# Attention of a mixture-of-experts layer: one stream of units, an order for each engine, and scores in two products

## What is computed

```python
x = x + attention(layernorm(x), ctx, mask)     # x 16x224x512, ctx 16x750x384, 8 heads of 64
x = x + ffn(layernorm(x))                      # 8 experts 512 -> 2048 -> 512, top 2, capacity 1120

q, k, v = x @ W_q, ctx @ W_k, ctx @ W_v
sim = where(mask, (q k^T) * 64**-0.5, -max)
out = softmax(sim) v @ W_o + b_o
```

## Time and profile before

| | us |
|---|---|
| median of 3 runs | 2237.76 (2236.44 to 2246.44) |
| the profiled execution | 2237.11 |
| its span | 2235.4 |
| PE busy in the span | 2096.5 (94%) |
| DVE, ACT, POOL busy | 996.3, 678.0, 488.8 |
| attention's logits finished at | 720.93 of the span |

### The profile page before, as it was taken

The page is one execution under the profiler, slowest core; times in us unless marked ns, Lnnn a source line. Parts: engine busy times, 40 slices in busy tenths (PEclk is TensorE's granted clock), DMA queues, the critical chain, the costliest instruction groups (busy, mean ns, idle before and its releaser), DMA issues.

```text
span 2235.4 us, 30763 instructions
## 1 busy us (share of the span) xinstructions
PE 2096.5 (94%) x12038; PEld 1860.0 (83%) x12038; DVE 996.3 (45%) x2223; ACT 678.0 (30%) x1672; POOL 488.8 (22%) x535
## 2 busy tenths in 40 slices
PE   3898998998897699999999999999999999999997
PEld 3777877877875599899989989998998999998997
DVE  4666766666655653422422342242224245234221
ACT  2633634634633222311321131132113124113110
POOL 0643643633633111111010111011111111111100
PEclk9999999999998699999999999999999999999999
DMA  4221121121111332510421251042124225123211
GB/s 131 63 81 50 31 80 44 36 80 38 43 50 57 119 102 64 144 28 19 136 65 15 48 152 36 14 124 70 28 48 137 53 55 154 28 47 115 38 15 15
DMA packets 95528, 148.32 MB, mean 66 GB/s; under 512 B 7920, under 2 KB 49312, under 8 KB 95376
## 3 DMA queue, kind: packets, MB, share of 16 engines
q1 hardware_dynamic: 79632, 109.36, 15.3%
q0 software_dynamic: 15744, 36.71, 9.3%
HBM read 110.66 MB, written 35.39 MB: 65 GB/s over the span
## 4 chain that ended last, share of the span: by engine, by line
PE 65%; DVE 1%; issue 0%; POOL 0%; POOLq 0%; ACT 0%; DVEq 0%
PE psH L1458 31%; PE psY L1458 31%; PE psX L1472 1%; PE psI L1514 1%; DVE w_lo L939 0%; PE psI L1504 0%; POOL out_dram L1274 0%; POOLq L1196 0%; DVE moves L1332 0%; DVE onehot L1340 0%; DVE psH L1410 0%; DVE hT_lo L1436 0%; DVE ys L1380 0%; DVE ys L965 0%; DVE eq_t L1323 0%
## 5 line engine op out<-in xcount | busy, mean ns | idle before, releaser
L1436 DVE SCALAR_TENSOR_TENSOR hT_lo<-psH,hT_hi 128x384 fp32r<-128x384 f32 (+1 forms) x384 | 209.9, 547 | 926.0 <-ACT hT_hi L1299 925.9
L1299 ACT ACTIVATE hT_hi<-psH 128x384 fp32r<-128x384 f32 (+1 forms) x384 | 185.4, 483 | 1112.4 <-PE psH L1458 1112.4
L1458 PE MATMUL psH<-xgT_hi,w_hi 128*128 128x384 f32 (+2 forms) x1536 | 484.3, 315 | 5.6 <-issue 5.4
L1458 PE MATMUL psH<-xgT_hi,w_lo 128*128 128x384 f32 (+2 forms) x1536 | 483.8, 315 | 0.0
L1458 PE MATMUL psH<-xgT_lo,w_hi 128*128 128x384 f32 (+2 forms) x1536 | 482.4, 314 | 0.0
L1458 PE MATMUL psY<-w_hi,hT_hi 128*128 128x512 f32 (+1 forms) x1002 | 403.1, 402 | 0.0
L1458 PE MATMUL psY<-w_lo,hT_hi 128*128 128x512 f32 (+1 forms) x1002 | 394.0, 393 | 0.4 <-issue 0.4
L1458 PE MATMUL psY<-w_hi,hT_lo 128*128 128x512 f32 (+1 forms) x1002 | 394.2, 393 | 0.0
L1458 PEld LDWEIGHTS psH<-xgT_hi,w_hi 128*128 128x128 f32 x1536 | 290.5, 189 | 28.4 <-issue 11.8
L1458 PEld LDWEIGHTS psH<-xgT_lo,w_hi 128*128 128x128 f32 x1536 | 290.6, 189 | 15.4
L1458 PEld LDWEIGHTS psH<-xgT_hi,w_lo 128*128 128x128 f32 x1536 | 290.3, 189 | 0.0
(11 more groups left out here) (188 smaller groups left out, 2939.2 us busy)
## 6 DMA issues: line engine op xcount, KB each, us to landing
stage<-in_L_ffn_W_dram SPq DMA_DIRECT2D x128, 512.0 KB, 4.5
x_sb<-in_x_dram SPq DMA_DIRECT2D x8, 896.0 KB, 7.9
x_res<-in_x_dram SPq DMA_DIRECT2D x8, 896.0 KB, 5.7
out_dram<-x_res SPq DMA_DIRECT2D x8, 896.0 KB, 4.8
xn_rows<-xn SPq DMA_DIRECT2D x8, 896.0 KB, 4.7
c_sb<-in_ctx_dram SPq DMA_DIRECT2D x16, 375.0 KB
out_dram<-zrow SPq DMA_DIRECT2D x9, 256.0 KB, 4.4
xg<-xn_rows,gid POOLq DMA_INDIRECT x72, 3.6
```

Source lines behind the costliest of these rows:

```text
L1299: nc.scalar.activation(hT[0][:, f % 2, 0:m], psH[f % 2][:, 0:m], ACT.Relu).then_inc(h_hi, 1)
L1436: nc.vector.scalar_tensor_tensor(out=hT[1][:, f % 2, 0:m], in0=psH[f % 2][:, 0:m], scalar=0.0, in1=f32(hT[0][:, f % 2, 0:m]), op0=ALU.max, ...
L1458: mm = nc.tensor.matmul(out, stationary(a, c), moving(b, c), start=first and c == chunks[0] and j == 0, stop=last and c == chunks[-1] and ...
```

## The change

Two things change together.

**Scores in two products.** q's hi part is written to both 64-row halves of its head's tile (ACT, two more instructions per `q`); the lo part stays in the head's own half, zeros in the other. k gets a tile for each head (`kz`), with the hi part in the head's own half and the lo part in the other one. Then q_hi over both halves times kz is hi·hi + hi·lo, and q_lo times kz is lo·hi: two matmuls for three. The split of `k` is two 64-row instructions on ACT and on DVE for one each.

**One stream of units.** Units 13 to 15 of a pair (`t-3` to `t-1`, `o-4` to `o-1`), its output projection and its whole tail move into the next pair's iteration, between that pair's units. Each engine gets a table of its own for the first pair, the loop, and the end. The function `iteration` is now called for pair 0, in the loop for 1 to 6, for 7, and once more for the tail of 7. The prologue makes only `fc`, `fx`, `k0` and `q0`; `v0` and `v1` move among the first units, and the weights W_v and W_o are split there (`w7` to `w13`). `tt` uses the ring's banks and no longer `psT`. SP stores the rows of pair p-1 within iteration p and then loads `xr` for pair p; POOL adds the bias late in the iteration, between units 11 and 15. The logits' transpose (`lt`) is a step of its own.

```diff
+PE_STEPS = order("""
+    t-3 q1 s0 k1 o-4 t-2 o-3 s1 s2 t-1 v0 s3 q2 o-2 o-1 t0 wo0 wo1 s4 v1 wo2 t1 v2 o0 v3 s5 o1 tt0 t2 t3
+    s6 s7 tt1 wo3 o2 t4 k2 o3 q3 t5 s8 k3 o4 t6 s9 s10 fc0 o5 tt2 t7 s11 tt3 fx0 o6 fx1 t8
+    s12 lg0 o7 fx2 t9 lt0 s13 o8 fc1 t10 fc2 o9 t11 s14 fx3 s15 k0 q0 o10 o11 t12
+""")
+ACT_STEPS = order("""
+    o-4 t-3 q1 k1 t-2 o-3 s0 v0 t-1 o-2 q2 o-1 s1 t0 s2 v1 s3 o0 v2 t1 v3 o1 t2 s4 s5 t3 s6 o2 t4 k2 o3
...
+""")
+POOL_STEPS = order("""
+    u0 fl0 u1 tl0 tl1 u2 u3 tl2 u4 u5 u6 tl3 u7 u8 u9 u10 u11 bi0 bi1 u12 u13 u14 bi2 bi3 u15
+""")
...
+PRO_ORDER = order("fc0 fc1 fc2 fx0 fx1 fx2 fx3 k0 q0")
...
@@ SP
+            def load_ahead(p):
+                sp.wait_ge(proj_mm, ring_start(p) - 2)
+                load_front(sp, T, A, p + 1)
+                sp.wait_ge(mbias, p + 1)
+                load_mask(p + 1)
+            def rows_out(p, prev, nxt):
+                sp.wait_ge(proj_done, ring(p, prev, nxt, "wo", TP - 1) + 1)
+                sp.dma_start(rows(A["out"][0:NTOK, :], p - 1), xr[:]).then_inc(x2_out, 16)
+                sp.wait_ge(xn2_done, TP * p)
+                sp.dma_start(rows(A["xn2"], p - 1), xn2[:]).then_inc(xn2_out, 16)
+                sp.wait_ge(x2_out, 16 * p)
+                held(sp, passed, xn2_out, 16 * p)
...
             with sp.Fori(1, NPAIR - 1) as p:
-                iteration(p, True)
+                load_ahead(p)
+                rows_out(p, True, True)
+                load_rows(p)
@@ ACT, split_hi
                 elif kind == "q":
-                    nc.scalar.activation(qz[0][0][0:64, i % 2, :], src[0:64, 0:TP * R], ACT.Copy)
-                    nc.scalar.activation(qz[1][0][64:128, i % 2, :], src[64:128, 0:TP * R], ACT.Copy).then_inc(proj_hi, 1)
+                    for h in range(2):
+                        nc.scalar.activation(qz[h][0][own[h], i % 2, :], src[own[h], 0:TP * R], ACT.Copy)
+                    for h in range(2):
+                        a = nc.scalar.activation(qz[h][0][own[1 - h], i % 2, :], src[own[h], 0:TP * R], ACT.Copy)
+                    a.then_inc(proj_hi, 1)
                 else:
-                    nc.scalar.activation(kT[0][:, i % 2, :], src[:, 0:TP * KC], ACT.Copy).then_inc(proj_hi, 1)
+                    for h in range(2):
+                        a = nc.scalar.activation(kz[h][own[h], i % 2, :], src[own[h], 0:TP * KC], ACT.Copy)
+                    a.then_inc(proj_hi, 1)
@@ DVE, split_lo
-                    a, h, o = src[:, 0:TP * KC], kT[0][:, i % 2, :], kT[1][:, i % 2, :]
+                    nc.vector.tensor_tensor(kz[0][64:128, i % 2, :], src[0:64, 0:TP * KC], f32(kz[0][0:64, i % 2, :]), ALU.subtract)
+                    a, h, o = src[64:128, 0:TP * KC], kz[1][64:128, i % 2, :], kz[1][0:64, i % 2, :]
@@ PE
                         for it in range(2):
                             at = b * S + it * R
-                            mm = product(psS[i % 2][0:R, it * NKEY:(it + 1) * NKEY],
-                                         lambda k, c: qz[h][k][:, hp % 2, at:at + R],
-                                         lambda k, c: kT[k][:, hp % 2, b * NKEY:(b + 1) * NKEY], 1)
+                            for k in range(2):
+                                mm = nc.tensor.matmul(psS[i % 2][0:R, it * NKEY:(it + 1) * NKEY], qz[h][k][:, hp % 2, at:at + R],
+                                                      kz[h][:, hp % 2, b * NKEY:(b + 1) * NKEY], start=k == 0, stop=k == 1,
+                                                      skip_group_check=True)
```

More of the change, by code:

```diff
@@ L159 @@
[L159 to L185, removed]
@@ new lines @@
+""")
+ACT_STEPS = order("""
+    o-4 t-3 q1 k1 t-2 o-3 s0 v0 t-1 o-2 q2 o-1 s1 t0 s2 v1 s3 o0 v2 t1 v3 o1 t2 s4 s5 t3 s6 o2 t4 k2 o3
+    s7 q3 t5 k3 s8 o4 fc0 t6 o5 t7 s9 fx0 fx1 t8 s10 s11 fx2 t9 o6 s12 fc1 fc2 o7 t10 t11 fx3 o8 o9
+    s13 k0 o10 s14 q0 o11 t12 s15
+""")
+DVE_STEPS = order("""
+    s0 t-3 o-4 q1 s1 k1 t-2 fs0 fs1 t-1 o-3 v0 o-2 fs2 fs3 q2 o-1 s2 wo0 fa0 wo1 t0 s3 o0 v1
+    s4 wo2 fp0 ap0 ap1 t1 v2 s5 v3 tt0 ap2 o1 t2 fp1 tt1 o2 fp2 s6 t3 wo3 t4 s7 k2 fp3 o3
+    s8 ap3 o4 q3 t5 k3 s9 fc0 tt2 t6 tt3 s10 fx0 s11 t7 s12 fx1 o5 o6 lg0 t8 lt0 fx2 t9
+    s13 fc1 fc2 t10 o7 fx3 s14 o8 s15 t11 o9 k0 mb0 o10 q0 t12 o11
@@ new lines @@
+""")
+POOL_STEPS = order("""
+    u0 fl0 u1 tl0 tl1 u2 u3 tl2 u4 u5 u6 tl3 u7 u8 u9 u10 u11 bi0 bi1 u12 u13 u14 bi2 bi3 u15
+""")
+PE_FIRST = order("""
+    s0 s1 q1 s2 k1 v0 s3 t0 v1 s4 t1 o0 v2 s5 t2 o1 v3 q2 s6 t3 o2 k2 s7 t4 o3 q3 s8 t5 o4 k3
+    s9 t6 fc0 o5 s10 t7 fc1 o6 fx0 s11 t8 o7 fc2 fx1 s12 t9 o8 fx2 s13 t10 o9 fx3 s14 t11 o10 k0 s15 t12 q0 o11
+""")
+ACT_FIRST = order("""
+    s0 w7 s1 w8 q1 w9 s2 k1 v0 t0 s3 v1 t1 s4 o0 w10 v2 t2 s5 o1 w11 v3 q2 t3 s6 o2 w12 k2 t4 s7 o3 w13 q3 t5 s8 o4 k3
+    t6 s9 fc0 o5 t7 s10 fc1 o6 fx0 t8 s11 o7 fc2 fx1 t9 s12 o8 fx2 t10 s13 o9 fx3 t11 s14 o10 k0 t12 s15 q0 o11
@@ new lines @@
+""")
+DVE_FIRST = order("""
+    s0 w7 s1 w8 q1 w9 s2 k1 v0 s3 t0 v1 s4 t1 o0 w10 v2 fs0 s5 t2 o1 w11 v3 fs1 q2 s6 t3 o2 w12 k2 fs2 fs3 s7 t4 fa0 o3 w13 q3
+    s8 t5 o4 k3 s9 t6 fc0 fp0 o5 fp1 s10 t7 fc1 fp2 o6 fp3 fx0 s11 t8 o7 fc2 fx1 s12 t9 o8 fx2 s13 t10 o9 fx3 s14 t11 o10 k0
+    s15 t12 mb0 q0 o11
+""")
+POOL_FIRST = order("u0 u1 u2 u3 u4 u5 u6 u7 fl0 u8 u9 u10 u11 bi0 u12 bi1 u13 bi2 u14 bi3 u15")
+PE_END = order("t-3 o-4 t-2 o-3 wo0 t-1 o-2 wo1 o-1 wo2 tt0 wo3 tt1 tt2 tt3 lg0 lt0")
+ACT_END = order("t-3 o-4 t-2 o-3 t-1 o-2 o-1")
@@ new lines, with steps, pe_steps @@
+DVE_END = order("t-3 o-4 t-2 o-3 wo0 t-1 o-2 wo1 o-1 ap0 wo2 ap1 tt0 wo3 ap2 tt1 ap3 tt2 tt3 lg0 lt0")
+RINGED = ("q", "k", "v", "fx", "fc", "wo", "tt", "lg")
+SPLIT = ("fx", "fc", "v", "q", "k")
+OF_NEXT = order("fx0 fx1 fx2 fx3 fc0 fc1 fc2 q0 k0 fs0 fs1 fs2 fs3 fa0 fp0 fp1 fp2 fp3 mb0 fl0")
+def steps(prev, nxt, first, middle, end):
+    if not prev:
+        return first
+    if nxt is None:
+        return end
+    return middle if nxt else [x for x in middle if x not in OF_NEXT]
+def pe_steps(prev, nxt):
+    return steps(prev, nxt, PE_FIRST, PE_STEPS, PE_END)
@@ L282, in load_mask, with load_rows @@
                     sp.dma_start(m_sb[:, b, :], m_row(p, b)).then_inc(m_in, 16)
[L284 to L300 removed]
+            def load_ahead(p):
[10 more added lines that the diff above has]
+                held(sp, passed, xn2_out, 16 * p)
+            def load_rows(p):
+                sp.dma_start(xr[:], rows(A["x"], p)).then_inc(xr_in, 16)
             load_mask(0)
```

344 lines of the change are left out of this document (189 added, 155 removed), and 3 rows, old and new, of the table ITER_ORDER.

## The result

The changed kernel takes 2173.6 us (median of four runs), the kernel before 2238.5 on the same chip: ratio 0.9706, 95% interval 0.9693 to 0.972. That is inside the stated range of 2136 to 2182, 64.9 us less where 88.4 were forecast, but outside the forecast's own 2136 to 2166. The profiled execution took 2173.7 us, its span is 2172.0.

A forecast was written before the change was run, and what follows sets the result against it. PE bounds attention: 73.7 us of work and 10.6 of gaps per 84.3 us pair. Prologue 46.5 + first 56 + loop 435 + last 65 + end 30 = 632.5 against 720.9, so 2149 us; own range 2136 to 2166, stated 2136 to 2182.

The forecast's parts named there:

- the first rival: Attention loop: gaps only shrink by half or less, 5.3 to 8 us a pair; 2172 to 2190 us, chance 0.24.
- Prologue: Work before the first scores `s0`: v0 and v1 leave, q0 slower, fewer memsets; 53.1 us becomes 46.5.
- Work 69.9: Loop pair: PE's work falls from 73.7 to 69.9 us, as 32 score matmuls at 0.118 us go (3.8).
- 2.6 us of gaps, a pair of 72.5: Loop pair in one stream: PE gaps shrink from 10.6 to 2.6 us, giving 72.5 us for 84.3.
- First iteration 56: Pair 0, from `s0` to the loop: 49.9 us of work plus 6 of waits while the pipe fills.
- the ring: Attention units: engine queues hold each other up in a circle, one unit in about 3 us where PE could do 2.2.
- The end 30: After the last iteration: tail of 24.6 us, leftover units' 4 and 1.5 of waits, 30 us.
- I leave their 1514 us alone: Experts' part behind the attention: same code, so its 1514 us stay as long as before.
- hidden by PE: Loop pair: ACT at 45.9 and DVE at 57.6 of 72.5 us, so their longer q and k copies cost nothing.
- the stream does nothing, only the products go: 2207: Rival, attention: all 10.6 us of gaps a pair stay, only the matmul saving counts; 2207 us, chance 0.09.
- The lock on DVE's xn2 (2163): Loop: DVE's xn2 normalization waits for POOL's products, 4 us more DVE a pair, half on the path; 2163, chance 0.15.
- The load of `xr` as the slower case: Loop, SP and POOL: `xr` lands too late for unit 12; 30 us late gives 2303 us, chance 0.03.

The follow-up runs named there:

- e13_oneorder: Changed kernel, but in its loop ACT and DVE follow PE's order of steps, PE's table unchanged: 2290.5 us, 1.022 of the kernel before.

## Why the prediction was right, and where it was not

- **The number: right, with some luck.** The loop came out 7 us better than forecast, and the first iteration, the end and the experts worse, so the time left the forecast's own range (2136 to 2166). It came to stand in the range of the first rival (2172 to 2190, gaps in the loop that only shrink), whose mechanism did not occur: the loop's pairs have no gaps. That the stated range reached up to 2182 for that rival is what took it in.
- **Prologue: right.** 46.5. With two memsets fewer beside it, the longest normalization of `x_sb` is 1.83 us for 3.40. The three sizes behind 46.5 (v's projections, q0 and k0, memsets) were not measured apart, and the runs with this same prologue start `s0` at 46.2 to 48.0, so that an error of 0 is partly luck.
- **"Work 69.9", "2.6 us of gaps, a pair of 72.5": the sum was near, the terms off.** Work is 71.0, gaps none. The score matmuls gave 3.4 and not 3.8; the other 0.7 I had missed in work counted by starts. The waits that I added for `lg0`, `s12` and `t4` did not occur.
- **"First iteration 56": wrong by 19, the step that failed.** I counted its work (49.9) and added 6 us of waits "while the pipe fills", without following its tables as I had the loop's. All four have nearly one order: the ring again. With tables like the loop's it is 57.0, so the size was right for a table that was not there. This term alone is 18.5 of the 25.0 us.
- **"The end 30": 34.5.** PE idles 8.3 us of it; the tail that I took over from before had 5.1, and I added 1.5. The last leftover units and output projections wait 0.85, 0.96 and 1.54 us for DVE, and the transposes 1.98 and 0.68 for `xn2`; some of the leftover units also run at the lower clock (an `o`'s matmuls start 0.21 us apart at 619 us, 0.11 at 625). The router's lower clock is no part of the miss: 5.60 us here, and 5.21 in the 24.6 that I took over.
- **"I leave their 1514 us alone": wrong by 7.7,** and told as a condition for being wrong. It is more than I would now leave out of a range.
- **ACT and DVE "hidden by PE": right in the stream,** where ACT's 6.7 us cost nothing. In the old order the same copies are not hidden. The rival "the stream does nothing, only the products go: 2207" had the sign wrong: had the stream done nothing, the run would have been 2314. I took a gap as a fixed amount beside PE's work; in the old order it grew from 7.5 to 14.9 us a pair when the work shrank, as in a ring whose own time counts and which the copies lengthen.
- **The lock on DVE's xn2 (2163) did not come, because the tables keep it apart, not because `xn2` is spared.** All 32 calls are short (min/median/max ns), and none of them ran beside a unit's product on POOL; those that ran beside POOL at all met its operations on one column:

```profile
L560 DVE TENSOR_SCALAR xn<-x_res,mv,rs x32: 514/540/549, 152.6 to 640.3; 112x512 f32<-112x512 f32 x32
L537 DVE TENSOR_SCALAR x_sb<-x_sb,mv,rs x32: 529/550/1827, 22.9 to 522.7; 112x512 f32<-112x512 f32 x32
```

 The same operation on `x_sb` met a product or a memset 15 times, and each of these calls took 0.90 to 1.83 us and ended 0.28 us behind POOL's instruction; the other 17 took 0.53 to 0.55. One of the 15, in order of time:

```profile
222.40 1.02 POOL L415 TENSOR_TENSOR probs<-probs,rsum 112x500 f32<-112x500 f32 x1
222.81 0.90 DVE L537 TENSOR_SCALAR x_sb<-x_sb,mv,rs 112x512 f32<-112x512 f32 x1
```

 The Trainium skill's "SBUF — State Buffer" (Who interferes with whom) has the second instruction wait for the first one's end; these rows agree. With one order in the loop (`e13_oneorder`) `xn2` does fall beside products, and 13 of its calls take 1.04 to 1.25 us:

```profile
L555 DVE TENSOR_SCALAR xn<-x_res,mv,rs x32: 515/544/1250, 157.9 to 755.0; 112x512 f32<-112x512 f32 x32
```

 That is some 1.2 us of DVE a pair, a small part of the 17.7 by which its pair is longer. So the mechanism behind the 2163 is real; what I had missed is that the order decides whether it strikes.
- **The load of `xr` as the slower case: no.** POOL no longer waits for it at all in this stage; the wait of 114.5 us in the earlier trace rows has gone.

## What to carry to other kernels

Before costing an edit at nothing because an engine is half idle, ask whether the engines follow one order: in such a ring a longer copy on an engine at 50% can be on the path, and may cost more than it saves. Let each engine take short steps that others wait for (a mask, an exponential) ahead of long copies that nobody needs yet, in a table of its own, and move whole tables, not single steps; here the same copies then cost nothing. Cost the first round of a software pipeline from its own table, step by step, not as the loop's work with an allowance. And before saying that a hold-up spares an operation, look in the trace for what ran beside it.

## What the hardware showed that was not expected

TensorE's granted clock falls over gaps of at most 2.3 us inside the work: with the products alone PE idles 14.9 us of a 92.3 us pair, none of the gaps longer than 2.32, and the mean clock is 0.94, part of the time at the lower of its two levels (1.2 and 2.4 GHz). It does not follow the idle time in sum: without q's second copies one pair idles 14.3 us at 1.00 and the next 12.7 at 0.94, with 3.5 us more of busy time for the same matmuls. In long straight code there are PE gaps of 0.2 to 4.4 us that wait for nothing in the profile's waits; those over 0.4 us end 1.2 to 1.6 us after a packet of instructions has landed, at places that move when instructions that never run are put ahead. Together with the clock behind them they make parts of 1514 to 1530 us out of the same work: a comparison of two kernels of this size can't tell 10 us of one part from where its code lies.
